# Experts of two tiles moved into the first half's chunks of an adaptive-norm FFN kernel

## The reference

```
w = weights[conditions]                       # (B, C, D) = (128, 32, 32)
hs = einsum('bct,bcd->bdt', x, w)             # hidden states, 256 wide
logits = hs @ gate_w                          # 8 experts
routing_weights, _ = top_k(logits, 2)
h = square(relu(hs @ up_w))                   # 256 -> 1024
y = h @ down_w + (hs @ expert_weight) * routing_weights.sum(-1, keepdims=True)
out = x + (y - mean(y)) * rsqrt(var(y) + 1e-5) * gamma + beta
```

## Time and profile before

| | |
|---|---|
| median of three runs | 229.4 us (229.4 to 229.56) |
| the profiled execution's own time | 229.29 us |
| its span in the profile | 227.6 us |
| TensorE matmul (PE) busy | 220.9 us, 97% of the span |
| TensorE weight load (PEld) busy | 191.4 us, 84% |
| VectorE (DVE) busy | 160.9 us, 71% |
| GpSimd (POOL) busy | 131.4 us, 58% |
| ScalarE (ACT) busy | 106.4 us, 47% |

### The profile page before, as it was taken

One profiled execution on the slowest core, in us unless ns is written; L12 is line 12 of the kernel. 1 busy time (PEld: TensorE's weight loads), 2 busy tenths in 40 slices (PEclk: granted clock), 3 DMA queues, 4 the chain that ended last, 5 costly groups with the idle time before them and its releaser, 6 DMA issues.

```text
span 227.6 us, 3998 instructions
## 1 busy us (share of the span) xinstructions
PE 220.9 (97%) x1260; PEld 191.4 (84%) x1260; DVE 160.9 (71%) x352; ACT 106.4 (47%) x187; POOL 131.4 (58%) x131
## 2 busy tenths in 40 slices
PE   7899999999999999999999999999999999999992
PEld 2798888888888889888889888888888888888892
DVE  6587965777667777667667766577766766777885
ACT  3379865444555345534545444544454444444000
POOL 3758795665545763656455764366555575557411
PEclk9999999999999999999999999999999999999999
DMA  3877123030603010000200002000020002000031
GB/s 98 231 213 230 50 59 103 10 98 7 187 10 98 9 66 30 0 0 3 92 0 0 3 0 95 3 0 0 0 95 1 0 0 68 28 0 0 10 108 69
DMA packets 17177, 11.81 MB, mean 52 GB/s; under 512 B 6660, under 2 KB 16900, under 8 KB 17156
## 3 DMA queue, kind: packets, MB, share of 16 engines
q1 hardware_dynamic: 15460, 10.43, 15.1%
q10 hardware_dynamic: 1280, 1.07, 1.4%
q0 software_dynamic: 416, 0.05, 0.2%
HBM read 7.35 MB, written 4.19 MB: 51 GB/s over the span
## 4 chain that ended last, share of the span: by engine, by line
PE 94%; DMA 1%; issue 1%; DVE 1%; ACTq 1%; POOLq 0%; POOL 0%; ACT 0%; DVEq 0%
PE up_ps L337 39%; PE down_ps L431 25%; PE down_ps L433 13%; PE hid_ps L303 5%; PE moe_ps L449 3%; PE moe_ps L448 3%; PE moe_ps L447 3%; DMA wd<-in_L_cond_weights_dram 1%; PE down_ps L303 1%; ACTq L513 1%; DMA cond_row<-in_itok_B_dram 1%; POOLq L46 0%; POOL rstd L697 0%; DVE result L615 0%; DVE stats L588 0%
## 5 line engine op out<-in xcount | busy, mean ns | idle before, releaser
L682 POOL TENSOR_TENSOR sq_lo<-square,sq_hi 128x512 fp32r<-128x512 f32 x64 | 84.4, 1322 | 77.0 <-DVE square L553 77.0
L431 PE MATMUL down_ps<-down_hl,sq_hi 128*128 128x512 f32 x248 | 88.8, 393 | 0.0
L553 DVE SCALAR_TENSOR_TENSOR square<-up_ps,relu 128x512 f32<-128x512 f32 x64 | 44.0, 687 | 37.3 <-ACT relu L491 28.2
L433 PE MATMUL down_ps<-down_hl,sq_lo 128*128 128x256 f32 x248 | 69.6, 280 | 0.0
L431 PEld LDWEIGHTS down_ps<-down_hl,sq_hi 128*128 128x128 f32 x248 | 46.5, 188 | 10.8 <-issue 0.3
L491 ACT ACTIVATE relu<-up_ps 128x512 f32<-128x512 f32 x64 | 38.2, 596 | 35.8 <-PE up_ps L337 35.7
L337 PE MATMUL up_ps<-hid_hi,up_hi 128*128 128x512 f32 (+1 forms) x136 | 52.8, 391 | 0.3 <-ACT hid_hi L476 0.3
L337 PE MATMUL up_ps<-hid_hi,up_lo 128*128 128x512 f32 (+1 forms) x136 | 51.1, 379 | 0.0
L433 PEld LDWEIGHTS down_ps<-down_hl,sq_lo 128*128 128x128 f32 x248 | 46.7, 188 | 2.4
L493 ACT ACTIVATE sq_hi<-relu 128x512 fp32r<-128x512 f32 x64 | 40.6, 634 | 2.0
L337 PE MATMUL up_ps<-hid_lo,up_hi 128*128 128x512 f32 (+1 forms) x136 | 40.6, 381 | 0.0
(11 more groups left out here) (62 smaller groups left out, 193.3 us busy)
## 6 DMA issues: line engine op xcount, KB each, us to landing
x_sb<-in_x_dram SPq DMA_DIRECT2D x7, 512.0 KB, 4.2
out_dram<-result SPq DMA_DIRECT2D x7, 512.0 KB, 3.0
wd<-in_L_cond_weights_dram SPq DMA_DIRECT2D x111, 4.0 KB, 1.5
x_sb<-in_L_ffn_down_w_dram SPq DMA_DIRECT2D x2, 512.0 KB, 4.7
x_sb<-in_x_dram ACTq DMA_DIRECT2D x2, 256.0 KB, 2.9
result<-in_L_ffn_up_w_dram ACTq DMA_DIRECT2D x2, 256.0 KB, 2.9
result<-in_L_ffn_up_w_dram SPq DMA_DIRECT2D x1, 512.0 KB, 4.7
out_dram<-result SPq DMA_DIRECT2D x4, 128.0 KB, 1.7
```

The source lines that it names most:

```text
L431: pe.matmul(dst[:, :], a_hi, down_hl[:, c, :, :].rearrange("p s t -> p (s t)"), start=(c == 0), stop=False)
L433: mm = pe.matmul(dst[:, T:2 * T], a_lo, down_hl[:, c, 0, :], start=False, stop=(c == CH - 1))
L553: dve.scalar_tensor_tensor(square[:, c % 2, :], up_ps[c % UPB][:, :], 0.0, relu[:, c % 2, :], ALU.max, ALU.mult).then_inc(square_done, 1)
L682: pool.tensor_tensor(sq_lo[:, j % 2, c, :], square[:, c % 2, :], sq_hi[:, j % 2, c, :].bitcast(f32), ALU.subtract).then_inc(sq_lo_done, 1)
```

## The change

`experts_at(0, c)` is empty now, and `first_chunks` calls `experts(0, 0)` and `experts(0, 1)`. `experts` does its `eg_hi` products first and those with `eg_lo` last. ACT loads the expert weights ahead of up part 1, POOL the gate weights as its first instruction, with a semaphore of its own. The rounding, the subtraction, the two gates and the two scalings move to earlier places of ACT's and DVE's programs.

```diff
@@ experts_at
             if j == 0:
-                return {4: [(0, 0)], 7: [(0, 1)]}.get(c, [])
+                return []
@@ sync
             load_up(sp, 2)
-            sp.dma_start(eg_raw[:, :, 0:T], expert_w.rearrange("(k p) h -> p k h", p=P)).then_inc(eg_landed, 16)
-            sp.dma_start(eg_raw[:, :, T:EG], gate_w.rearrange("(k p) e -> p k e", p=P)).then_inc(eg_landed, 16)
@@ first_chunks
                 first_rest(1, 0)
-                first_rounded(2, 0)
+                experts(0, 0)
                 conditioning_first(1)
-                first_rest(2, 0)
-                first_rounded(3, 0)
-                first_rest(3, 0)
+                for c in range(2, FIRST):
+                    first_rounded(c, 0)
+                    first_rest(c, 0)
+                experts(0, 1)
@@ experts
-                if j == 0 and t == 0:
+                first = j == 0 and t == 0
+                if first:
                     pe.wait_ge(eg_hi_ready, 1)
-                    pe.wait_ge(eg_lo_ready, 1)
...
-                    pe.matmul(dst, a_hi, eg_lo[:, k, :], start=(k == 0), stop=False)
+                    pe.matmul(dst, a_hi, eg_hi[:, k, :], start=(k == 0), stop=False)
                     pe.matmul(dst, a_lo, eg_hi[:, k, :], start=False, stop=False)
-                    mm = pe.matmul(dst, a_hi, eg_hi[:, k, :], start=False, stop=(k == K - 1))
+                if first:
+                    pe.wait_ge(eg_lo_ready, 1)
+                for k in range(K):
+                    a_hi = hid_hi[:, par, k, P * t:P * t + P]
+                    mm = pe.matmul(dst, a_hi, eg_lo[:, k, :], start=False, stop=(k == K - 1))
@@ scalar
             split_up(0)
+            act.dma_start(eg_raw[:, :, 0:T], expert_w.rearrange("(k p) h -> p k h", p=P)).then_inc(eg_landed, 16)
             load_up(act, 1)
             load_x_first(act, 1)
             hidden_first(0, 0)
             hidden_first(0, 1)
+            act.wait_ge(eg_landed, 16)
+            act.wait_ge(gate_landed, 16)
+            act.activation(eg_hi[:, :, :], eg_raw[:, :, :], ACT.Copy).then_inc(eg_hi_ready, 1)
             split_up(1)
+            scale_moe(0, 0)
             hidden_first(1, 0)
             hidden_first(1, 1)
...
                     rectify(j, c)
                     if j == 0 and c == 0:
-                        act.wait_ge(eg_landed, 32)
-                        act.activation(eg_hi[:, :, :], eg_raw[:, :, :], ACT.Copy).then_inc(eg_hi_ready, 1)
+                        scale_moe(0, 1)
@@ vector
             hidden_first(0, 1)
+            dve.wait_ge(eg_hi_ready, 1)
+            dve.tensor_tensor(eg_lo[:, :, :], eg_raw[:, :, :], eg_hi[:, :, :].bitcast(f32), ALU.subtract) \
+                .then_inc(eg_lo_ready, 1)
             split_up(1)
+            gate(0, 0)
             hidden_first(1, 0)
             hidden_first(1, 1)
             dve.wait_ge(up_landed[2], 16)
             dve.tensor_copy(up_hi[:, :, split_cols(2)], up_raw[:, :, split_cols(2)]).then_inc(up_hi_ready, 1)
+            gate(0, 1)
             split_up(2)
...
-                    if j == 0 and c == 0:
-                        dve.wait_ge(eg_hi_ready, 1)
-                        dve.tensor_tensor(eg_lo[:, :, :], eg_raw[:, :, :], eg_hi[:, :, :].bitcast(f32), ALU.subtract) \
-                            .then_inc(eg_lo_ready, 1)
@@ gpsimd
+            pool.dma_start(eg_raw[:, :, T:EG], gate_w.rearrange("(k p) e -> p k e", p=P)).then_inc(gate_landed, 16)
             pool.memset(minus_half[:, :], -0.5).then_inc(consts_ready, 1)
```

More of the change, by code:

```diff
@@ L111, in adaln_ffn @@
         down_landed = [sem(f"down_landed{n}") for n in range(DOWN_LOADS)]
-        eg_landed, ln_landed = map(sem, ("eg_landed", "ln_landed"))
+        eg_landed, gate_landed, ln_landed = map(sem, ("eg_landed", "gate_landed", "ln_landed"))
         cond_first_landed, cond_later_landed = map(sem, ("cond_first_landed", "cond_later_landed"))
```

## The result

The changed kernel takes 230.98 us (median of six runs, 230.83 to 231.41) against 229.40 (229.26 to 229.78): ratio 1.0059, 95% interval 1.0048 to 1.007. It is slower by 1.4 us by the ratio (1.6 between the medians), between the prices of rivals A (230.2) and B (231.4) and outside the range. The profiled execution took 230.96 us, span 229.3.

A forecast was written before the change was run, and what follows sets the result against it. TensorE, busy 97% of the span, was taken as the bound, with no named wait after 7.74 us. Terms of -0.08 us and four zeros gave -0.1: span 227.5, 229.2 with 1.7 around it, forecast 229.3 us, range 228.9 to 230.4.

The forecast's parts named there:

- A: Rival: x of the second half lands late, TensorE waits before the second half's conditioning; 230.2 us, chance 0.17.
- B: Rival: POOL's gate load takes over 2.8 us, a hole over 0.5 us before the same conditioning; 231.4 us, chance 0.07.
- Second half of x: Its load, third on ACT's queue, was taken to land at 9.6 us, wanted at 9.85: no hole, bounds 0 and 1.25 us.
- the slow microsecond: 8.20 to 9.20 us, DMA engines at only 63 GB/s as SP's up part 2 started; 1.0 us in x's upper bound.
- Table rows of the second half: Rows for the second conditioning: SP's last at 9.15 us, POOL's by 8.8; a hole of 0.05 us possible, none taken.
- Block 1: Later stage: conditioning inputs in time, ACT some 0.7 us late at chunk 5, tightest slack 0.9 us; cost taken as zero.
- new order of TensorE: `experts(0, 0)` from 9.23 us, second half's conditioning 9.95, `experts(0, 1)` 12.25, second half 12.97, `up(0, 4)` possible at 15.80.
- `eg_hi` and `eg_lo` in time: Expert weights' rounded part ready at 8.6 us, needed 9.23; rest at 9.35, needed 9.71: slack 0.4, no hole.
- POOL's gate load: Gate weights first on POOL from 0.9 us: 1 us taken, 0.56 to 4.5 possible, effect on table rows taken as 0.
- the first square in time: DVE's first square ahead of `up(0, 4)`: ends at 15.45 us, wanted at 15.75, slack 0.3.
- rival D: TensorE waits for `eg_lo` or the first square, up to 0.3 us; counted inside the forecast, together 0.68.
- hole of 0.08 us: Old order's TensorE wait for the first square ahead of `up(0, 4)`; the new order closes it, -0.08 us, bounds 0 and +0.3.

The follow-up runs named there:

- e5: Changed kernel, with SP waiting until the expert weights have landed before it issues up part 2, about 1 us later; 229.60 us, ratio 1.0003.
- e11: As e6, but SP waits for the first rounded hidden part instead of the expert weights before it issues up part 2; 229.91 us, ratio 1.0015.
- e3: Changed kernel, with SP waiting until x of the second half has landed before it issues up part 2; 230.22 us, ratio 1.0034.
- e7: Changed kernel, with SP's up part 2 in two loads of 256 columns, pieces of 1 KB instead of 2 KB; 230.32 us, ratio 1.0029.
- e2: Kernel before, with only the expert and gate weight loads moved as in the change, experts where they were; 231.06 us, ratio 1.0057.
- e4: Changed kernel, with x of the second half second and up part 1 third on ACT's queue; ratio on record 1.0103, profiled execution 229.90 us.
- e6: As e5, and DVE takes gate(0, 2) ahead of the square of chunk 1 of block 1; 229.72 us, ratio 1.001.
- e8: As e5, with tile 1's experts, gate and scaling back at chunk 7, only tile 0's early; 230.04 us, ratio 1.0025.
- e1: Changed kernel, with ACT's expert load issued ahead of its table rows; 231.35 us, ratio 1.0063.
- e9: Changed kernel, with the expert load on POOL behind the gate weights instead of on ACT, and e6's gate move; 231.54 us, ratio 1.0077.
- e10: Kernel before, with only the expert and gate weight loads taken from SP to POOL's start; 232.06 us, ratio 1.0098.

## Why the prediction was wrong

**The step that failed** is "Second half of x". It named the input that decides, its third place, the slow stretch beside it and a latest landing of 11.1 us, and then took 9.6, "near the queue's own pace, on which both rows of that queue agree: no hole". Measured: 11.29, beyond the upper end too. The two rows were of loads that had all but ended when SP's part 2 started to move (14 of ACT's pieces left at 8.09); they could say nothing of a load that meets it. The earlier trace rows was read as a slow stretch of the DMA engines and given to the bound alone. It was none: in the same stretch after, 312 GB/s moved. What costs is the taking of turns with SP's pieces, and on the last DMA engine it cost more than the bound allowed. And a mean pace is the wrong measure: thirteen of sixteen shares kept it, and the semaphore waits for the last one. A had the right place and mechanism, with 0.17, but for its evidence it too leaned on the slow microsecond; its price of 230.2 was too low, since it took the middle of the landings left (10.8) and nothing in block 1.

**Table rows of the second half**, a second term taken as nothing. The prediction said that waiting out one load more would put SP's last at 9.9, a hole of 0.05, and took none. It landed at 10.05, and in e5 and e11, where x was in time, at 10.02 and 10.17: a hole of about 0.2 to 0.3 us, which x hides in the changed kernel.

**The mechanism** is shown by its removal from two sides: SP 1.1 us later (e5) or after x (e3), landing 9.85 and 9.70; SP's pieces halved (e7), 10.44 and half of the loss. That the loads alone do it is e2. The Trainium skill's "DMA: Bandwidth & Descriptors", queues, rings and completion order, has the engines take turns between queues packet by packet; e3, e5 and e7 agree with it. The Trainium skill's page puts typically 9 to 17 descriptors in a packet; here a turn was a single piece, since x's last ones stood an even 0.122 us apart. Why it is three or four shares that stay behind, and not all, no run here settles. The tail goes with the number of ACT's pieces left when SP's first one starts: 114 and 124 (the changed kernel and e2), 74 in e7, 69 in e4, which had none, 42 in e11 and 20 or fewer in e5 and e6.

**Block 1**, which the prediction cost at nothing ("have tile 1's gate behind them"), lost 0.35 us. The look at ACT and DVE was right in sign, but POOL's chain was left out: its squares' rests run back to back, they start with the first square, 1.4 us later in the new order, and in block 1 a DVE square waits for them with a gate queued behind it. e11 against e5 shows it for the gate, to the greater part; e3, e6 and e8 have no loss either, but there TensorE was held up by 0.3 to 0.7 us at `up(0, 4)` first.

**The spread 0.17 us** was not in the prediction either, which took the reordering inside `experts` as free. Its cause stays open.

**Right**: the new order of TensorE up to 9.83 us to 0.02; `eg_hi` and `eg_lo` in time (8.08 to 8.72 and 8.76 to 9.47); up part 1 (0.6 us later than said, inside its slack); POOL's gate load at 0.91 us for 1, and B's fall; the first square in time in the changed kernel and e5 (in e3, e6 and e8, with part 2 landing at 13.36 or later, it was not: rival D's wait). The hole of 0.08 us was under-sized. What goes is 0.26: after a TensorE pause the next matmul's distance is 0.31 instead of 0.23 us as well, and the group at 16.69 no longer waits for block 1's rows. With x in time, e5 took 229.60 us beside 229.52 of the kernel before, where the sum had 0.1 less than before. That it comes so near is in part luck: by its trace 0.2 us were lost at the conditioning, 0.4 in block 1 and 0.16 spread, and 0.27 won at the holes.

## What to carry to other kernels

A load moved to the front of a queue is paid by the last load of that queue, and its landing must be worked out against whatever other queues move at that time, by its slowest share and not by the mean pace: before trusting the queue's own rows, look whether any of them met the same neighbour. Where TensorE has next to no holes, reordering its work can win only those (0.26 us here), so each input with under 1 us of slack is a risk and not a detail. And when work is put ahead of the first product that a back-to-back engine waits for, follow that engine's chain to its end, with everything queued behind the waits for it.

## What the runs showed of the hardware that was not expected

Table rows of 4 KB suffer much from a large load set in motion before them: 256 KB, on ACT's queue at 1.95 us (e1) or on POOL's at 2.35 (e9, e10), moved the last landing of the first half's rows from 6.63 us to between 7.60 and 7.71. (In e1 ACT also issued its own rows 0.3 us later.) TensorE's pauses ahead of and between the two pairs of conditioning matmuls, 1.1 and 0.5 us in e10, were followed by a granted clock of 0.50, its lower level of 1.2 GHz, from 7.86 to 11.28 us. So in that execution a late start cost 1.1 us by itself and as much again by pace: the lag at the first `up_ps` matmul was 1.1 us, eleven matmuls later 2.2. Two loads on different queues took turns piece by piece on the slowest DMA engine: 0.042 us from piece to piece alone, 0.085 beside pieces of 1 KB and 0.122 beside pieces of 2 KB.
